# Long filter: half of the values of three batches loaded during the projections in place of seven Toeplitz groups

## What is computed

```python
v = jax.nn.silu(_causal_dwconv(x @ Wv, conv_v))
vh = v.reshape(b, l, H, DV)
fs = _fir(vh, fir_short)          # 3 taps
fl = _fir(vh, fir_long)           # 31 taps
...
o = p[..., 0:1] * fs + p[..., 1:2] * fl + p[..., 2:3] * delta
```

## Time and profile before

| | |
|---|---|
| median of 3 runs | 2634.45 us (2634.22 to 2636.96) |
| the profiled execution's own time | 2633.81 us |
| its span in the trace | 2632.1 us |
| granted TensorE clock, mean | 0.961 |
| PE busy | 2427.5 us (92%) |
| DVE busy | 1657.0 us (63%) |
| ACT busy | 1108.4 us (42%) |
| POOL busy | 629.4 us (24%) |
| conv_heads, from its first load to the end | about 115 to 442 us |
| long_filter, up to the first instruction of the next stage | 442 to 555.6 us |

### The profile page before, as it was taken

How to read it: one execution, slowest core, us unless ns; L and a number is a source line. 1 busy time by engine, 2 the same in 40 slices (tenths; PEclk the granted TensorE clock), 3 DMA queues, 4 the chain that set the end, 5 groups by cost and what they waited for, 6 DMA issues and landing times.

```text
span 2632.1 us, 39930 instructions
## 1 busy us (share of the span) xinstructions
PE 2427.5 (92%) x13580; PEld 1690.8 (64%) x13580; DVE 1657.0 (63%) x4351; ACT 1108.4 (42%) x2285; POOL 629.4 (24%) x422
## 2 busy tenths in 40 slices
PE   6799995566998999989999999999999999999998
PEld 4466664555787888845665666666666656666665
DVE  4487874449922566535666675767667676766665
ACT  2478874446663222224333424432343334234331
POOL 2145544131101111211212231222123132312210
PEclk9999998787898999989999999999999999999999
DMA  5456565878777767421201120221022022101000
GB/s 171 152 162 192 175 196 170 236 217 206 210 173 209 226 193 236 153 84 37 57 6 51 57 58 1 57 57 28 29 58 57 1 56 57 42 15 56 9 9 8
DMA packets 393199, 274.10 MB, mean 104 GB/s; under 512 B 216610, under 2 KB 350690, under 8 KB 390802
## 3 DMA queue, kind: packets, MB, share of 16 engines
q1 hardware_dynamic: 388370, 245.95, 32.9%
q0 software_dynamic: 4640, 25.73, 3.0%
HBM read 170.70 MB, written 100.93 MB: 103 GB/s over the span
## 4 chain that ended last, share of the span: by engine, by line
PE 46%; DVE 6%; issue 2%; POOL 2%; ACT 0%; DVEq 0%; ACTq 0%; POOLq 0%
PE mx_up L1960 18%; PE mx_dn L1974 17%; PE mx_m L1910 4%; DVE mx_acc L2288 2%; PE mx_m L1937 2%; POOL mx_rms L1866 2%; PE mx_m L1914 1%; PE mx_m L1951 1%; DVE hl L2171 1%; DVE hl L2160 1%; DVE mx_rms L2165 1%; PE mx_m L1930 1%; PE mx_m L1919 1%; PE mx_m L1945 1%; PE mx_m L1924 1%
## 5 line engine op out<-in xcount | busy, mean ns | idle before, releaser
L2288 DVE SCALAR_TENSOR_TENSOR mx_acc<-mx_dn,mx_comb,mx_acc 128x256 f32<-128x256 f32 x1024 | 424.4, 477 | 370.3 <-PE mx_dn L1974 367.5
L1960 PE MATMUL mx_up<-mx_h2T,mx_eup 128*128 128x512 f32 x1024 | 494.3, 606 | 0.0
L1974 PE MATMUL mx_dn<-mx_edn,mx_hs 128*128 128x256 f32 x2048 | 487.7, 381 | 0.0
L1974 PEld LDWEIGHTS mx_dn<-mx_edn,mx_hs 128*128 128x128 f32 x2048 | 385.5, 190 | 146.4 <-issue 87.9
L2062 ACT ACTIVATE mx_hs<-mx_up 128x512 f32<-128x512 f32 x320 | 190.9, 597 | 611.3 <-PE mx_up L1960 610.6
L1960 PEld LDWEIGHTS mx_up<-mx_h2T,mx_eup 128*128 128x128 f32 x1024 | 192.5, 193 | 158.7 <-issue 148.6
L666 DVE SCALAR_TENSOR_TENSOR cv_acc<-cv_pre,conv_w,cv_acc 128x512 f32<-128x512 f32 x288 | 215.6, 750 | 78.3 <-ACT cv_acc L588 71.4
L530 PE MATMUL cv_pj<-cv_hT,wqkv 128*128 128x512 f32 x384 | 181.7, 603 | 12.8 <-ACT cv_acc L588 7.8
L700 POOL TENSOR_TENSOR rn<-cv_ss,half_pow 128x8 f32 x64 | 127.5, 1992 | 13.2 <-POOL cv_ss L696 13.2
L1852 POOL TENSOR_TENSOR mx_st<-mx_tmp,root_pow 128x24 f32<-128x24 f32 x30 | 124.6, 4170 | 20.4 <-DVE mx_tmp L2114 20.4
L1974 PEld LDWEIGHTS mx_dn<-mx_sdn,mx_hs 128*128 128x128 f32 x512 | 97.3, 190 | 40.5 <-issue 30.6
(11 more groups left out here) (294 smaller groups left out, 4042.5 us busy)
## 6 DMA issues: line engine op xcount, KB each, us to landing
kqT_d<-cv_kqc SPq DMA_DIRECT2D x16, 1024.0 KB, 8.6
vf_d<-cv_vf SPq DMA_DIRECT2D x16, 1024.0 KB, 5.2
fl_toep<-taps_d SPq DMA_DIRECT2D x32, 392.0 KB, 6.9
ds_kqT<-kqT_d SPq DMA_DIRECT2D x10, 1024.0 KB, 5.7
fl_v<-vf_d SPq DMA_DIRECT2D x8, 1216.0 KB
ci_kT<-kqT_d POOLq DMA_DIRECT2D x19, 512.0 KB, 6.1
fl_d<-fl_out POOLq DMA_DIRECT2D x8, 1029.0 KB, 7.8
xin<-_attn_hidden_states_dram SPq DMA_DIRECT2D x16, 512.0 KB, 4.1
```

Of the source, the lines that this page charges most:

```text
L1960: ins = pe.matmul(up_ps[x % 2][:], lhs, h2T[i][:, k, :], start=(k == 0), stop=(k == KD - 1))
L1974: ins = pe.matmul(dn_ps[(i + n) % 2][:, j, :], hs[x % 4][:, j * P:(j + 1) * P], rhs, start=(x == 0 and j % 2 == 0) or x >= NS, stop=(x >= ...
L2288: ins = dve.scalar_tensor_tensor(out=acc[i][:, j, :], in0=dn_ps[(i + n) % 2][:, j, :], scalar=comb[i][:, j, e:e + 1], in1=acc[i][:, j, :], ...
```

## The change

The tile `v`, its zeroed corners and the loads of half 0 for batches 0, 1 and 2 move into the time of conv_heads. Only RT0 = 6 of the 13 Toeplitz tiles exist there; the other 7 are allocated and filled in long_filter. POOL's memsets stand at the start of conv_heads. At units 7, 11 and 15 SP waits for the stores of the finished batch and issues its three loads, between `load(u)` and `put(u - 2)`. In long_filter SP loads batch 3 and then Toeplitz groups 6 to 12, and goes on as before. Each turn of half 0 is cut in two: 63 windows (batches 0 to 2) at once, 21 windows (batch 3) when they have landed. Half 1 is turned as before.

```diff
@@ conv_heads, SP
             for u in range(2, NU):
                 load(u, u % 2)
-                if u - 2 < RT:
+                if u - 2 < RT0:
                     load_toep(sp, m, u - 2)
+                if u % UB == UB - 1 and u >= 2 * UB - 1:
+                    b = u // UB - 1
+                    if b == 0:
+                        sp.wait_ge(m.v_zero, 2 * B)
+                    for i in two:
+                        sp.wait_ge(store[i], 32 + 32 * (b + 1) * UB // 2)
+                    load_v(sp, m, 0, b, m.v_first)
                 put(u - 2, u % 2)
             for i in two:
                 put(NU - 2 + i, i)
+            sp.wait_ge(m.v_first, 16 * 3 * (B - 1))
@@ conv_heads, POOL
+            for b in range(B):
+                pool.memset(m.v[0:32, b * NW, :], 0.0).then_inc(m.v_zero, 1)
+                pool.memset(m.v[96:P, b * NW + NW - 1, :], 0.0).then_inc(m.v_zero, 1)
+            pool.wait_ge(m.v_zero, 2 * B)
@@ long_filter
-        v = sb("fl_v", [P, NA, HC])
+        v = m.v
+        m.toep += [sb(f"fl_toep{i}", [P, TC, WIN]) for i in range(RT0, RT)]
...
+        early, late = slice(0, (B - 1) * NW), slice((B - 1) * NW, NA)
@@ long_filter, SP
-            sp.wait_ge(zero_done, 2 * B)
-            for b in range(B):
-                load_v(0, b)
-
+            load_v(sp, m, 0, B - 1, v_in[0])
+            for g in range(RT0, RT):
+                load_toep(sp, m, g)
             sp.wait_ge(act_turned, 1)
             sp.wait_ge(dve_turned, NV - 1)
@@ long_filter, ACT (DVE in the same way, for its three pieces)
+                if hf == 0:
+                    turn(early)
+                    act.wait_ge(v_in[0], 16 * 3)
+                    turn(late).then_inc(act_turned, 1)
+                else:
+                    act.wait_ge(v_in[1], 16 * 3 * B)
                     act.wait_ge(mm_done, GH)
-                turn(hf)
+                    turn(slice(0, NA)).then_inc(act_turned, 1)
@@ long_filter, DVE, half 0
+                    for k in ks:
+                        turn(k, early)
+                    dve.wait_ge(v_in[0], 16 * 3)
+                    for k in ks:
+                        turn(k, late).then_inc(dve_turned, 1)
@@ build
-        m.toep = [mid.enter_context(nc.sbuf_tensor(f"fl_toep{i}", [P, TC, WIN], F32)) for i in range(RT)]
+        m.toep = [mid.enter_context(nc.sbuf_tensor(f"fl_toep{i}", [P, TC, WIN], F32)) for i in range(RT0)]
+        m.v = mid.enter_context(nc.sbuf_tensor("fl_v", [P, B * NW, D // 2], F32))
```

More of the change, by code:

```diff
@@ L32 @@
 RT = 13
+RT0 = 6
 TAPROW = P + WIN - 1
@@ L710, in load_toep, with load_v, tokens @@
     sp.dma_start(m.toep[g % RT][:], rows).then_inc(m.toep_in[g % RT], 16)
+def load_v(sp, m, hf, b, done):
+    row, half, first = 2 * D, D // 2, WIN - FIRL + 1
+    def tokens(t0, n, rows):
+        return bass.AP(tensor=m.vf_d.tensor, offset=(b * L + t0) * row + hf * half,
+                       ap=[[row, rows], [WIN * row, n], [1, half]])
+    o = m.v[:, b * NW:(b + 1) * NW, :]
+    last = L - (NW - 1) * WIN + FIRL - 1
+    sp.dma_start(o[:, 1:NW - 1, :], tokens(first, NW - 2, P)).then_inc(done, 16)
+    sp.dma_start(o[FIRL - 1:, 0:1, :], tokens(0, 1, WIN)).then_inc(done, 16)
+    sp.dma_start(o[0:last, NW - 1:NW, :], tokens((NW - 1) * WIN - FIRL + 1, 1, last)).then_inc(done, 16)
 def long_filter(nc, m, w):
@@ L719, in long_filter @@
     NA = B * NW
-    LAST = L - (NW - 1) * WIN
-    HALO = FIRL - 1
     XG = CF // TC
@@ L737, in long_filter @@
         ps = [ctx.enter_context(nc.psum_tensor(f"fl_ps{i}", [P, 2, 512], F32)) for i in range(RP)]
-        zero_done = sem("fl_zero_done")
         v_in = [sem(f"fl_v_in{i}") for i in two]
@@ L745, in long_filter, with turned @@
         block = ctx.enter_context(nc.Block("long_filter"))
[L747 to L755, removed]
+        def turned(k, n=slice(0, NA)):
+            return vc[:, k * CF:(k + 1) * CF, n].rearrange("p c n -> p n c"), v[:, n, k * CF:(k + 1) * CF]
+        early, late = slice(0, (B - 1) * NW), slice((B - 1) * NW, NA)
         @block.gpsimd
         def _(pool):
-            for b in range(B):
-                pool.memset(v[0:32, b * NW, :], 0.0).then_inc(zero_done, 1)
-                pool.memset(v[96:P, b * NW + NW - 1, :], 0.0).then_inc(zero_done, 1)
             for y in range(NX // XG):
@@ L785, in _ @@
             for b in range(B):
-                load_v(1, b)
+                load_v(sp, m, 1, b, v_in[1])
                 sp.wait_ge(mm_done, b + 1)
@@ L824, in _, with turn @@
         def _(act):
-            def turn(hf):
-                out, src = turned(TURNED_BY_ACT)
-                act.activation(out, src, ACT.Copy).then_inc(act_turned, 1)
+            def turn(n):
+                out, src = turned(TURNED_BY_ACT, n)
+                return act.activation(out, src, ACT.Copy)
             for hf in two:
-                act.wait_ge(v_in[hf], 16 * 3 * B)
-                if hf:
+                if hf == 0:
[4 more added lines that the diff above has]
+                    act.wait_ge(v_in[1], 16 * 3 * B)
                     act.wait_ge(mm_done, GH)
-                turn(hf)
+                    turn(slice(0, NA)).then_inc(act_turned, 1)
                 for x in range(hf * NX // 2, (hf + 1) * NX // 2, 2):
@@ L843, in _, with turn @@
         def _(dve):
-            def turn(k):
-                out, src = turned(k)
-                dve.tensor_scalar(out, src, 1.0, None, ALU.mult).then_inc(dve_turned, 1)
+            def turn(k, n):
+                out, src = turned(k, n)
+                return dve.tensor_scalar(out, src, 1.0, None, ALU.mult)
+            ks = [k for k in range(NV) if k != TURNED_BY_ACT]
             for hf in two:
-                dve.wait_ge(v_in[hf], 16 * 3 * B)
-                if hf:
+                if hf == 0:
+                    for k in ks:
[3 more added lines that the diff above has]
+                        turn(k, late).then_inc(dve_turned, 1)
+                else:
+                    dve.wait_ge(v_in[1], 16 * 3 * B)
                     dve.wait_ge(mm_done, GH)
-                for k in range(NV):
-                    if k != TURNED_BY_ACT:
-                        turn(k)
+                    for k in ks:
+                        turn(k, slice(0, NA)).then_inc(dve_turned, 1)
                 for x in range(hf * NX // 2 + 1, (hf + 1) * NX // 2, 2):
@@ L2381, in build @@
         mid = ctx.enter_context(ExitStack())
-        m.toep = [mid.enter_context(nc.sbuf_tensor(f"fl_toep{i}", [P, TC, WIN], F32)) for i in range(RT)]
+        m.toep = [mid.enter_context(nc.sbuf_tensor(f"fl_toep{i}", [P, TC, WIN], F32)) for i in range(RT0)]
+        m.v = mid.enter_context(nc.sbuf_tensor("fl_v", [P, B * NW, D // 2], F32))
+        m.v_zero = mid.enter_context(nc.semaphore("fl_zero_done"))
+        m.v_first = mid.enter_context(nc.semaphore("fl_v_first"))
         m.toep_in = [mid.enter_context(nc.semaphore(f"fl_toep_in{i}")) for i in range(RT)]
```

## The result

| | before | changed |
|---|---|---|
| median of 20 runs each | 2635.04 us (2631.33 to 2649.89) | 2621.56 us (2615.66 to 2633.25) |
| ratio, 95% interval | | 0.9944 (0.9931 to 0.9956) |
| the profiled execution: time, span | 2633.81, 2632.1 us | 2633.25, 2631.5 us |

By the ratio the change takes off 14.8 us (11.6 to 18.2), more than the 0.2% that counts as no change. The forecast was 17.8 us, 2616.6 us.

What follows compares the result with a forecast made beforehand. SP's transfer stream was taken to bound the filter: 2.0 (memsets) + 15.6 (three batches) + 8.7 (gap) + about 2 (second start) - 10.1 (seven groups) = 18.2. It took 17.8 us off, giving 2616.6 us, range 2612 to 2625.

Steps and rivals of the forecast that it cites:

- rival A: Toeplitz groups 6 to 12 in the filter cost 2.0 us each or more; gain 11 to 14 us; chance 0.15.
- three signs of being wrong: In the filter: a DMA gap stays, Toeplitz issues exceed 2 us before the first store, or PE waits for groups 6-12.
- Memsets: POOL's eight memsets move to the start of conv_heads at no cost; SP starts 2.0 us earlier in the filter.
- The turns: Half 0 in the filter: DVE's three early turns take 7.0 us beside batch 3's load; PE starts 19.6 us earlier.
- Toeplitz groups 6 to 12: Seven groups in SP's filter stream, 1.44 us each from start to start; PE does not wait for them.
- Half 1's values: In the filter, the 8.7 us wait goes; first issue 20.4 us earlier, landing 17.8 us earlier, the number handed on.
- rival B: First three stores in the full queue delay Toeplitz groups 13 to 15 more; at 3 us each, gain 9; chance 0.08.
- the price of a batch: Loads of v: 5.2 us a batch in the steady stream; batch 3 alone lands 7.2 us after its first issue.
- rival D: The tile's early life moves every early-stage buffer, or the 63-window turns wait for something; 2630 to 2637 us; chance 0.04.
- What follows, moved only: Filter from half 1's stream on keeps order and prices; the store issue of 8.78 us beside DVE's turn stays.
- In conv_heads: Early batches cost nothing: the kqT store at unit 7 has 17.4 us of slack against 5.2 us of batch.
- Rival C: At units 7, 11, 15 batches push the kqT store past ACT's silu; 0.2% slower at 25 us each; chance 0.03.

Runs made afterwards that it cites:

- pe_late: Changed kernel with 20 useless PE matmuls ahead of group 0; stage 98.9 us, median 2621.26 us, ratio to before 0.9949.
- aligned: Changed kernel with pads of 192 bytes ahead of v and 64 behind, so v starts on a multiple of 256; stage 94.6 us, median 2617.16 us.
- groups_late: Changed kernel, but all four batches of half 0 loaded in the filter and turned whole, seven Toeplitz groups behind; stage 118.7 us, median 2640.26 us.
- before_shifted: Kernel before, with v moved 64 bytes off its multiple of 256 by pads; stage 120.3 us, median 2643.78 us, ratio 1.0041.
- early_x3: Changed kernel with two extra reads of 19 windows to spare HBM behind each early batch; conv_heads 326.0 us, median 2622.05 us, ratio 0.9937.
- early_x6: Changed kernel with five extra reads of 19 windows to spare HBM behind each early batch; conv_heads 346.3 us, median 2644.22 us, ratio 1.0024.

## Why the prediction held, and what was off

*The range and the forecast.* The median of 2621.56 us lies in the whole range, 2612 to 2625, but not in the forecast's own, 2613.5 to 2619.5, which had the chance of 0.70; by the ratio the gain is 14.8 us (11.6 to 18.2), where the forecast had 15 to 21. The whole range reached so far for the rivals, A (2621 to 2623.5, dearer Toeplitz groups) above all. A did not happen; a price that no rival named, of nearly the same size (about 4 us), took its place. So the steps below were mostly right, and that the number still fell into the range was in part luck. None of the three signs of being wrong came: no DMA gap stayed, the first seven issues of the Toeplitz line took 1.54 us each, and PE ran groups 0 to 13 (x224) without a wait.

*What bounds.* Right. The stage's length followed SP's stream in every run, and did not follow PE's start (pe_late).

*Memsets.* Right; the stage starts with SP's issue, and conv_heads is not longer.

*The turns.* Three early ones took 6.56 us (7.0 foreseen), the three late ones 2.36 (2.9). They lie where they were put, and PE's first matmul came 9.0 us after the barrier (8.1).

*Toeplitz groups 6 to 12.* 1.44 us foreseen, 1.54 measured from issue to issue, and 1.39 in aligned. So the lower price was right, and rival A (2.0 or more) did not come. By the rule of the Trainium skill that the prediction weighed ("DMA: Bandwidth & Descriptors", Specifications) the 392-byte pieces should have been no cheaper than those of 512. The traces do not bear that out: 1.39 us for 1024 pieces are 1.4 ns each, and a piece of the values was 1.94 ns in before.

*Half 1's values.* The wait for the turns and the gap of 8.7 us are gone, as foreseen: the DMA shares of the first two stretches are 1.02 and 0.98. The first issue came at 13.6 us after the barrier, 13.0 foreseen. The number handed on was 17.8 us; half 1's turn in fact starts 15.9 us earlier. From half 1's first issue to its turn it was 36.5 us in before, 40.4 in the changed kernel and 37.7 in aligned; the prediction's numbers give 36.5 + 20.4 - 17.8 = 39.1. So rival B, the stores in a full queue, did not come either: with v where it had been, that stretch was shorter than foreseen.

*The step that was mis-sized is the price of a batch*, "in the steady stream it costs 5.2 us". That held for v where it was in before. The change allocates v in another place, 64 bytes past a multiple of 256, and there a batch costs 6.0 us (groups_late, before_shifted). A batch alone shows the same: batch 3 was to land 7.2 us after its issue; it took 8.1 us in the changed kernel and 7.2 in aligned. Five batches stay in the stage, 5 x 0.8 = 4 us, and the stage is 98.8 us where 113.6 - 17.8 = 95.8 was foreseen; the other terms came out 1 us better than the sum. With v back on its multiple the stage is 94.6, a gain of 19.0 by the same steps. The sum had listed that every buffer of the early stages moves, in rival D, and took it for a risk to those stages. conv_heads did not mind; the tile that was moved did.

The Trainium skill has a sentence near this, in "DMA: Bandwidth & Descriptors", section "How a descriptor splits into AXI transactions": transfers are cut into transactions of 256 bytes, and each must start on a multiple of 256. It speaks of reading; here the reads were the same and the written address moved. Worked out from its rule, as an estimate, a 512-byte piece takes two transactions from a multiple of 256 and three from 64, 128 or 192 bytes past one. The cost in the runs was the same at the three as well: 5.97 us a batch at 192 and 5.99 at 64, and at 128 the stage and the landing of batch 3 as at 64. The page's count of beats would differ between the three, which the runs don't show. That an extra transaction is the mechanism stays an argument; that the start address is the cause is shown both ways, by aligned and before_shifted.

*What follows, moved only.* Nearly. Behind half 1's turn came 44.8 us, 43.7 before. The store whose issue had taken 8.78 us beside DVE's turn now came 1 us ahead of the turn (497.35) and took 0.52. That gained nothing: in aligned it fell beside the turn again (493.66, 8.76 us), and behind the turn's start came 44.1 us.

*In conv_heads.* The cost was nothing, as foreseen. At unit 7 the batch held SP for 7.0 us instead of 5.2, against 17.4 of slack. In early_x3 SP was held for 12.3 us (234.84 to 247.09) without a loss, in early_x6 for 23.4 (233.69 to 257.13), and there the kernel was 0.24% slower than before. By the slack of 17.4 us that is 3 x (23.4 - 17.4) = 18 us to be lost; conv_heads lost 20. Rival C had put the point at 25 us for 0.2%; its mechanism was sized about right, and its condition is far off.

*From the stage to the median.* 14.8 us in the stage, 14.8 by the ratio (11.6 to 18.2). The median is 5.0 us above the forecast: 3.0 are the stage, and 2.0 lie within the spread of the stages behind it (below).

## What to carry to other kernels

When a change moves a buffer that DMAs fill, look at where it now starts: a tile filled in 512-byte pieces cost 15% more per batch off a multiple of 256 bytes, and a pad mended it. Sum a stage's stream with its empty stretches as terms of their own: a transfer put into a gap cost nothing here (six groups, 0.1 us, less than two profiles of one kernel differ by), and one taken out of a full stream paid only until the next wait, the turns, came last. Where one kernel's profiles differ by more than the change, compare the stage that was edited.

## What was not expected of the hardware

- **The start of the written tile.** Batches of 2680 packets of 512 bytes (nearly all) from HBM: 5.2 us each with the tile on a multiple of 256 bytes, 6.0 us at 64 or 192 bytes past it. A batch alone landed after 7.2 us on a multiple of 256 and after 8.1 at 64 or 128 bytes past it.
- **Two lengths of one stage.** delta_scan, which no kernel here changes, took 305.6 to 306.2 us in eight profiles and 315.5 to 315.7 in six, nothing between. In ten-microsecond windows of the first profile of the changed kernel the granted clock is at the lower level (0.50) for the first 30 us of the stage, and in its second profile back at the upper one after the first ten:

```profile
816.70:826.70 10.00, 7.95 (x57) 6.53 (x57) 3.12 (x8) 0.38 (x1) 3.36 (x8) 0.50 0.87 266
826.70:836.70 10.00, 10.00 (x61) 8.75 (x62) 3.46 (x10) 1.18 (x5) 2.32 (x4) 0.50 1.03 308
836.70:846.70 10.00, 10.00 (x65) 8.75 (x62) 3.02 (x8) 1.18 (x5) 2.32 (x4) 0.50 0.03 7
```

```profile
812.30:822.30 10.00, 7.96 (x62) 6.56 (x62) 3.54 (x9) 0.38 (x1) 3.35 (x8) 0.58 0.87 260
822.30:832.30 10.00, 10.00 (x114) 8.75 (x114) 5.83 (x16) 2.36 (x10) 2.32 (x4) 1.00 1.05 317
```

PE is busy all of the second window in both, with 61 matmuls in the one and 114 in the other, so the 10 us are matmuls at half the clock. The three longest runs of the changed kernel (2630.3 to 2633.3) have the lowest mean clocks (0.952 or 0.953). What decides between the two was not tried and stays open.
